# Layer norms and a projection in column tiles, the bf16 terms of the roots moved between partitions by small transfers

## The reference, cut to what matters

```
x += conv0(x)              # routed 1x1 conv, 3x3 depthwise, 1x1 conv (96 hidden channels)
x += conv1(x)
y  = layernorm(x);  x += attention(y)
y  = layernorm(x);  x += ffn0(y)         # 5/2-bit float operands
y  = layernorm(x);  x += fourier(y)      # 48 hidden; FFT over 3136 tokens, complex diagonal, ReLU, inverse, projection to 24
y  = layernorm(x);  x += ffn1(y)
layernorm(x) = (x - mean_c(x)) / sqrt(var_c(x) + 1e-5)      # over the 24 channels of a token
```

## Time and profile before

| | us |
|---|---|
| median of 3 runs | 2803.33 |
| lowest, highest run | 2799.18, 2808.28 |
| profiled execution, its time | 2798.5 |
| profiled execution, its span | 2796.5 |
| mean granted TensorE clock | 0.896 |

### The profile page before, as it was taken

The page is one execution under the profiler, slowest core; times in us unless marked ns, Lnnn a source line. Parts: engine busy times, 40 slices in busy tenths (PEclk is TensorE's granted clock), DMA queues, the critical chain, the costliest instruction groups (busy, mean ns, idle before and its releaser), DMA issues.

```text
span 2796.5 us, 46610 instructions
## 1 busy us (share of the span) xinstructions
PE 2463.6 (88%) x18624; PEld 1413.1 (51%) x18624; DVE 1950.9 (70%) x3622; ACT 1682.0 (60%) x2834; POOL 70.6 (3%) x123
## 2 busy tenths in 40 slices
PE   3867988999979998999989998999989998987776
PEld 1323433666436744664436644466436744673562
DVE  4765877785957887797866786876857888355243
ACT  2334445765667577765666567665667667657534
POOL 1000000000000000000000000000000000000000
PEclk9977989998989999999969998999979999787865
DMA  4001000100020001000010001000010000000000
GB/s 133 1 1 18 1 1 1 19 1 1 1 35 2 2 1 29 8 1 1 10 26 2 1 1 31 5 2 1 1 25 2 1 1 18 1 1 4 15 1 18
DMA packets 108582, 29.63 MB, mean 11 GB/s; under 512 B 104144, under 2 KB 104272, under 8 KB 107984
## 3 DMA queue, kind: packets, MB, share of 16 engines
q1 hardware_dynamic: 108368, 26.65, 4.7%
HBM read 17.00 MB, written 9.63 MB: 10 GB/s over the span
## 4 chain that ended last, share of the span: by engine, by line
PE 66%; DVE 15%; ACT 14%; issue 4%; SPq 1%; DMA 0%; ACTq 0%; DVEq 0%
PE P L664 12%; PE P L645 10%; PE P L709 7%; PE P L679 6%; PE P L857 4%; PE P L700 4%; DVE acc L1348 4%; PE P L898 4%; PE P L685 3%; PE P L870 3%; ACT H L1016 2%; PE P L882 2%; PE P L810 2%; DVE SQ L1483 1%; PE P L725 1%
## 5 line engine op out<-in xcount | busy, mean ns | idle before, releaser
L1348 DVE SCALAR_TENSOR_TENSOR acc<-H,Dm,acc 128x784 f32<-128x784 f32 x1024 | 991.6, 1026 | 119.9 <-ACT acc L1024 119.5
L645 PE MATMUL P<-T,Wk 96*128 96x448 f32 (+1 forms) x768 | 409.9, 618 | 68.5 <-ACT H L1016 46.5
L664 PE MATMUL P<-H,diag 64*64 64x392 f32 x4608 | 403.9, 500 | 1.5 <-ACT H L1016 0.8
L1016 ACT ACTIVATE H<-P,biasA 128x448 f32<-128x448 f32 (+1 forms) x384 | 238.6, 621 | 258.9 <-PE P L645 209.4
L664 PEld LDWEIGHTS P<-H,diag 64*64 64x64 f32 x4608 | 172.0, 135 | 214.8 <-issue 207.2
L709 PE MATMUL P<-T,pack_b 96*96 96x448 f32 x448 | 245.0, 638 | 34.1 <-DVE T L1444 19.0
L645 PEld LDWEIGHTS P<-T,Wk 96*128 96x128 f32 x768 | 132.5, 207 | 216.1 <-ACT H L1016 122.0
L679 PE MATMUL P<-acc,Wk 128*96 128x392 f32 x512 | 200.2, 538 | 14.6 <-ACT acc L1053 14.5
L1047 ACT ACTIVATE acc<-P,biasT 128x392 f32<-128x392 f32 x128 | 68.4, 584 | 204.1 <-PE P L664 204.0
L882 PE MATMUL P<-pack_b,arena 128*96 128x112 f32 x928 | 118.4, 280 | 30.7 <-DVE arena L1483 17.3
L679 PEld LDWEIGHTS P<-acc,Wk 128*96 128x96 f32 x512 | 87.3, 178 | 111.8 <-issue 111.2
(11 more groups left out here) (198 smaller groups left out, 4156.8 us busy)
## 6 DMA issues: line engine op xcount, KB each, us to landing
xin<-in_x SPq DMA_DIRECT2D x224, 42.0 KB, 2.2
out_y<-arena SPq DMA_DIRECT2D x8, 1176.0 KB, 5.7
pack_b<-in_pack_b SPq DMA_DIRECT2D x1, 3820.0 KB, 17.9
arena<-in_pack_s SPq DMA_DIRECT2D x1, 1780.0 KB, 9.0
pack_a<-in_pack_a SPq DMA_DIRECT2D x1, 1084.0 KB, 5.2
pack_i<-in_pack_i SPq DMA_DIRECT2D x1, 318.0 KB, 2.9
arena<-in_pack_k SPq DMA_DIRECT2D x1, 192.0 KB, 3.1
```

Source lines behind the costliest of these rows:

```text
L645: pe.matmul(conv_rows(slice(0, 128), H1B, m), Wk1[:, 128 * (u % NT):128 * (u % NT + 1)], image_rows(T[q % 3], a + r0, m), start=True, stop ...
L664: last = pe.matmul(conv_rows(slice(64 * h, 64 * (h + 1)), CVB + r, HH), diag[64 * r:64 * (r + 1), tap, :], H1[64 * r:64 * (r + 1), slot(s, ...
L1016: act.activation(H1[:, slot(s, j), o + r0:o + r0 + m, 1:1 + HW], conv_rows(slice(0, 128), H1B, m), ACT.Relu, bias=biasA[:, j, 1:2]).then_i ...
L1348: ins = ve.scalar_tensor_tensor(a, H1[:, slot(s, j), r:r + SR, c:c + HW], Dm[:, j, tap:tap + 1], a, ALU.mult, ALU.add)
```

## The change

- A variance chunk is four matmuls of 32 weight columns and 112 moving columns, into the four groups of 32 PSUM partitions. The variances of a norm stand as 128 x 112, and so do the root, the reciprocal and the three terms.
- The terms are no longer moved by VectorE. SyncE moves each of the three terms with four transfers (32 partitions x 112 bf16 values each) into `thirds`, 96 x 448: term k in partitions 32k to 32k+31. A chunk's spread is one bf16 matmul with 96 weight rows and 448 moving columns, and it waits for all twelve transfers.
- The projection of a frequency and image pair is two matmuls, of 64 and of 56 weight columns and 48 moving columns each, into PSUM partitions 0 to 63 and 64 to 119. A group holds 5 frequencies, so there are 6 groups for 8. `S2` and the constant `g` have 120 rows for 112.
- SyncE's program has the same three streams as the other engines and an order of its own in `TURNS`. The orders of all engines are written anew (TensorE's has 1508 turns for 1398, VectorE's 744 for 801, ScalarE's 1256 for 1211).
- GpSimd no longer clears four small buffers at the start. The pack with `selb` is smaller.

```
-LB = 14
-LN_N = TOK // LB
+LT = 4
+LN_N = CK // LT
+KR = 64 + HW
...
 TURNS = {
+    "sync": (
+        "d7 c11 m3 c3 m3 b3 c4 m2 c1 m1 c2 m3 b7 c4 m3 c3 b3 m3 b4 c4 m3 c3 b3 m3 b4 c4 m3 c3 b3 m3 b4 c4 m3 "
+        "c3 m3 b7 c3 m3 b3 m3 b4 m3 b3 m3 b8 "
+    ),
...
-        NX, NA, NW, NBI, NTR, NFO = 14, 12, 8, 8, 6, 7
+        NX, NA, NW, NBI, NTR, NFO = 14, 12, 6, 8, 6, 7
-            KG, KP = 4, 120
+            KG = 5
...
         @block.sync
+            def load(n):
+                if n >= XG:
+                    sp.wait_ge(in_tp.sem, n - XG + 1)
...
+            def conv_part(q):
+                for g in range(NCK):
+                    if q * NCK + g >= XG:
+                        yield
+                        load(q * NCK + g)
...
+            def shift_terms(q, norm, chain, before):
+                for k, made in enumerate((2, 4, 5)):
+                    yield
+                    sp.wait_ge(chain.sem, chain.at(q, before + made))
+                    for t in range(LT):
+                        sp.dma_start(norm.thirds[32 * k:32 * (k + 1), t, :],
+                                     norm.terms[k][32 * t:32 * (t + 1), :]).then_inc(norm.thirds_moved.sem, 16)
+            def middle(q):
+                yield from shift_terms(q, normM, chain_m, 0)
+                yield from shift_terms(q, normM, chain_m, 5 + 4)
+            def back(q):
+                yield from shift_terms(q, normB, chain_b, 0)
+                yield from shift_terms(q, normB, chain_b, 5 + NSG)
+                yield
+                sp.wait_ge(ot_ready.sem, ot_ready.at(q, NCK))
+                sp.dma_start(out_v[bass.ds(q * QI, QI), :, :].rearrange("b p f -> p b f"), xout).then_inc(out_stored.sem, 16)
...
                 def variance(c):
-                    for t in range(2):
-                        sq = LN_N * ((2 * c + t) % 4)
-                        last = pe.matmul(P[64 * t:64 * (t + 1), norm.var, 0:LN_N], par["selv"][0:R, o:o + 64],
+                    for t in range(LT):
+                        sq = CK * (c % 2) + LN_N * t
+                        last = pe.matmul(P[32 * t:32 * (t + 1), norm.var, 0:LN_N], par["selv"][0:R, o:o + 32],
                                          norm.SQ[:, sq:sq + LN_N], start=(c == 0), stop=(c == NCK - 1))
...
-                        pe.wait_ge(norm.rs_ready.sem, norm.rs_ready.at(q, i + 1))
+                        pe.wait_ge(norm.thirds_moved.sem, norm.thirds_moved.at(q, (i + 1) * 3 * LT * 16))
...
-                    for h in range(2):
-                        dst = P[0:R, norm.spread[c % NSP], LN_N * h:LN_N * (h + 1)]
-                        pe.matmul(dst, selb16[:, 2 * c + h, :], norm.rb2, start=True, stop=False)
-                        last = pe.matmul(dst, selb16[:, 2 * c + h, :], norm.rb3, start=False, stop=True)
-                    last.then_inc(norm.rs_psum.sem, 1)
+                    pe.matmul(P[0:R, norm.spread[c % NSP], 0:CK], selb16[0:96, c, :], norm.thirds[:, :, :].rearrange("p t n -> p (t n)"),
+                              start=True, stop=True).then_inc(norm.rs_psum.sem, 1)
...
-                            o = KP * (k % KG) + 2 * CH * j
-                            last = pe.matmul(P[0:2 * HW, B0 + g % BN, o:o + 4 * CH].rearrange("p (a n) -> p a n", a=2), UV[:, 2 * k + j, :],
-                                             twice, start=True, stop=True)
+                            o = R * (k % KG) + 2 * CH * j
+                            for p, a, n in ((0, 0, 64), (64, HW, HW)):
+                                last = pe.matmul(P[p:p + n, B0 + g % BN, o:o + 2 * CH], UV[:, 2 * k + j, a:a + n],
+                                                 par["fw2"][0:R, :], start=True, stop=True)
...
-                rest, third = norm.sdev, norm.rstd
-                link(ve.tensor_copy(norm.rb2, norm.rstd), q, half)
-                link(ve.tensor_tensor(rest, norm.rstd, norm.rb2, ALU.subtract), q, half)
-                link(ve.tensor_copy(norm.rmid, rest), q, half)
-                for h in range(2):
-                    ve.tensor_copy(norm.rb2[64 * h + 32:64 * h + 60, :], norm.rmid[64 * h:64 * h + 28, :])
-                link(ve.tensor_tensor(third, rest, norm.rmid, ALU.subtract), q, half)
-                ve.tensor_copy(norm.rb3[0:32, :], third[0:32, :])
-                ve.tensor_copy(norm.rb3[64:96, :], third[64:96, :]).then_inc(norm.rs_ready.sem, 1)
+                rest, (high, middle_, low) = norm.sdev, norm.terms
+                link(ve.tensor_copy(high, norm.rstd), q, half)
+                link(ve.tensor_tensor(rest, norm.rstd, high, ALU.subtract), q, half)
+                link(ve.tensor_copy(middle_, rest), q, half)
+                link(ve.tensor_tensor(low, rest, middle_, ALU.subtract), q, half)
```

More of the change, by code:

```diff
@@ L214, in __init__, with small @@
         self.n, self.D, self.SQ, self.cen, self.var, self.spread = n, D, SQ, cen, var, spread
+    def small(self, room, thirds):
+        self.sdev, self.rstd = room[:, 0:LN_N], room[:, LN_N:2 * LN_N]
+        terms = room[:, 2 * LN_N:2 * LN_N + 3 * LN_N // 2].bitcast(BF16)
+        self.terms = [terms[:, LN_N * k:LN_N * (k + 1)] for k in range(3)]
+        self.thirds = thirds
 class Ffn:
@@ L316, in build @@
         normM = Norm(n=0, D=Yf, SQ=z[0:R, 0:2 * CK], cen=(3,), var=4, spread=(3, 4))
[L317 to L320 removed]
+        normM.small(z[:, 2 * CK:], sb("thirdsm", [96, LT, LN_N], BF16))
         YT = z[0:BLK, 0:2 * BPG * (R + 1)].rearrange("p (b n) -> p b n", b=2 * BPG)
@@ L330, in build @@
         normB = Norm(n=2, D=Y, SQ=SQ[0:R, :], cen=(5, 6), var=7, spread=(5, 6, 7))
-        roots = sb("roots", [128, 2 * LN_N])
-        normB.sdev, normB.rstd = roots[:, 0:LN_N], roots[:, LN_N:]
-        normB.rmid = SQ[:, 0:LN_N // 2].bitcast(BF16)
-        normB.rb2, normB.rb3 = (sb(name, [128, LN_N], BF16)[:, :] for name in ("rb2b", "rb3b"))
+        roots = sb("roots", [128, CK])
+        normB.small(roots, sb("thirdsb", [96, LT, LN_N], BF16))
         T = Ts
@@ L426, in build @@
             norm.sd_ready = sig(f"deviation_ready_{half}", layers)
-            norm.rs_ready = sig(f"rstd_ready_{half}", layers)
+            norm.thirds_moved = sig(f"rstd_terms_moved_{half}", layers * 3 * LT * 16)
             norm.rs_psum = sig(f"rstd_in_psum_{half}", layers * NCK)
@@ L518, in _, with conv_end @@
         def _(sp):
-            def load(q, groups):
-                for g in groups:
-                    n = q * NCK + g
-                    if n >= XG:
-                        sp.wait_ge(in_tp.sem, n - XG + 1)
-                    o = BPG * (n % XG)
-                    for i in range(QI):
-                        src = x_v[q * QI + i, :, BPG * CH * g:BPG * CH * (g + 1)].rearrange("p (j c) -> p j c", c=CH)
-                        dma = sp.dma_start(xin[:, o:o + BPG, CH * i:CH * (i + 1)], src)
-                        dma.then_inc(xin_loaded[n % XG].sem, 16)
-            def store(q):
+            def load(n):
+                if n >= XG:
+                    sp.wait_ge(in_tp.sem, n - XG + 1)
+                o, g = BPG * (n % XG), n % NCK
+                for i in range(QI):
+                    src = x_v[n // NCK * QI + i, :, BPG * CH * g:BPG * CH * (g + 1)].rearrange("p (j c) -> p j c", c=CH)
+                    dma = sp.dma_start(xin[:, o:o + BPG, CH * i:CH * (i + 1)], src)
+                    dma.then_inc(xin_loaded[n % XG].sem, 16)
+            def conv_part(q):
[3 more added lines that the diff above has]
+                        load(q * NCK + g)
+            def conv_end(q):
+                yield
[12 more added lines that the diff above has]
+                yield from shift_terms(q, normB, chain_b, 5 + NSG)
+                yield
                 sp.wait_ge(ot_ready.sem, ot_ready.at(q, NCK))
@@ L536, in _ @@
                 sp.dma_start(pack_t[key], packs[key]).then_inc(par_loaded[key].sem, 16)
-            load(0, range(XG))
+            for n in range(XG):
+                load(n)
             for key in ("a", "s", "b"):
                 sp.dma_start(pack_t[key], packs[key]).then_inc(par_loaded[key].sem, 16)
-            for q in range(NQ):
-                load(q, range(XG, NCK))
-                if q + 1 < NQ:
-                    load(q + 1, range(XG))
-                if q >= 2:
-                    store(q - 2)
-            for q in range(max(NQ - 2, 0), NQ):
-                store(q)
+            for_quads("sync", conv_part, conv_end, middle, back)
             sp.wait_ge(out_stored.sem, 16 * (NQ + 1))
@@ L884, in fourier @@
                     last.then_inc(sp_psum.sem, 1)
-                twice = par["fw2"][0:R, :].unsqueeze(1).broadcast_to([R, 2, 2 * CH])
                 for g in range(NW):
@@ L911, in fourier @@
                         o = 2 * HW * (k % 4)
-                        last = pe.matmul(P[0:R, B0 + g % BN, o:o + 2 * HW], S2[:, k, :], par["g"][0:2 * HW, k, :],
+                        last = pe.matmul(P[0:R, B0 + g % BN, o:o + 2 * HW], S2[:, k, :], par["g"][0:KR, k, :],
```

(13 more changed lines are left out.)

30 lines of the change are left out of this document (13 added, 17 removed), and 213 rows, old and new, of the table TURNS.

## The result

The changed kernel takes 2868.84 us (median of 4 runs, 2865.96 to 2875.54) beside 2801.73 us for the kernel before on the same chip: a ratio of 1.0224, 95% interval 1.0191 to 1.0256. It is slower by 67 us by the medians and by 63 us by the ratio, where 2700 us were forecast. The profiled execution takes 2875.54 us, with a span of 2873.8.

The account below looks back on a forecast made before the run. TensorE was taken as nearly the bound (88% busy, 66% of the chain). Its matmuls -104, VectorE's norm work -14, late terms +14 us: -104 from 2798.5, forecast 2700 us, 8-in-10 range 2655 to 2780.

Parts of the forecast that it names:

- Rival (c): Terms come late and TensorE stands at each norm's first spread matmul: up to 157 us lost, 2842 us; chance 0.09.
- (d): With less to do, TensorE's mean granted clock falls by 0.02, costing 37 us: 2737 us; chance 0.10.
- the one on the root: Reciprocal to spread: VectorE's savings give 14 us; transfers add 3.6 us, bare in the last quad's four norms, 14 us lost.
- SyncE's queue: Input loads behind a norm's terms come at most some us late, covered by the ring of four chunks: no cost.
- The sum: TensorE's busy time falls by 54 (projection), 47 (spread) and 34 us (variances), 135 us together.
- The variances' term: Variance chunks as eight instructions, four at a time: 0.24 us for 0.38, saving 34 us at the mean clock.
- The projection's term: Projection as 1856 short matmuls at 30.0 ns, 56 us for 112.6: a saving of 54 us.
- L870's 30.0 ns: Time per instruction of an existing two-tile matmul (64 weight, 58 moving columns), taken as the new projection's price.
- Rival (a): Short matmuls are not cheap: projection at 63 ns an instruction, 32-column tiles only two at a time; 2771 us, chance 0.10.
- The 77%: Share of TensorE's 135 us saving that becomes time, midway between 66% of chain and 88% busy: 104 us.
- Rival (b): Co-bound: VectorE or ScalarE fill in, 0.4 of TensorE's 135 us is realised, 54 us: 2750 us; chance 0.16.
- the 15/70 of the step: VectorE's chain share over its busy share, turning 64 us less VectorE work in the norms into 14 us.

Follow-up runs that it names:

- experiment 1: Changed kernel with its new orders, the twelve transfers a norm replaced by twelve VectorE copies: 2733.67 us, ratio 0.9763.
- experiment 2: Kernel before with its own orders, plus the change's variances, spread and projection in tiles (groups of 4) and twelve VectorE copies: 2769.95 us, ratio 0.9890.
- experiment 3: Changed kernel with only the first term moved, by four transfers a norm, the second and third left out of the result: 2704.72 us, ratio 0.9659.
- experiment 7: Changed kernel with SyncE moving only the first term; VectorE copies the second and subtracts the third straight into place: 2732.98 us, ratio 0.9739.
- experiment 6: Changed kernel without transfers: VectorE copies the first two terms and subtracts the third straight into place: 2736.04 us, ratio 0.9753.

## Why the prediction was wrong

Rival (c) is what happened, with (d) on top. The step that failed is the one on the root: "TensorE has other streams' work in front of the wait as long as three quads are under way, and that hides it. It is bare where one quad's chain sets the end."

- **The cover.** The step took 4 of 32 norms as bare. In the trace TensorE waits in 31 of 32. Other streams' work does lie around, but TensorE executes its list strictly in order, and the list holds too little of it between the last variance and the first spread of a norm. The trace of the kernel before could have told this, norm by norm. There the spread starts 4.2 us after the reciprocal at the least, 5.3 us at the median, and later than 9.1 us in only 3 of the 32 norms. The step's own middle, 4.2 + 3.6 = 7.8 us, is later than 26 of them. Had each of these been held back to 7.8 us, that would be 65 us in all, and to 9.1 us 101 us (estimates, from the intervals in that trace), where the step took 14. The prediction never made this count, which is what decides (c).
- **The price.** The interval was to be 6.5 to 9.1 us, and 9.85 was measured. The step had 0.33 to 0.53 us an issue and eleven issues in a row. The rows of after have 7.47/12 = 0.62 us from one to the next. Landing was 1.7 us, near its bound of 1.8. So 5.65 us more in the last norm, where 3.6 was taken and 4.9 was the far end. Four norms of it are 23 us and would have been inside the range; 32 of them are 181 us. The waits for the terms grew by 127.9 us (19.0 to 146.9), so some 30% of it was covered.
- **SyncE's queue.** "An input load that stands behind a norm's terms comes at most some us late" looked at the wrong side. The terms stand behind the loads, and in the norm at 1221.51 the interval grew to 14.0 us by it. This is in five of the middle program's norms only, some 14 us beyond 9.9 us in all.
- **The clock.** (d) had a fall of 0.02, 37 us. The fall was 0.04, and the step in (d) named less work as the cause. With less work alone it fell by 0.015 (experiment 1). The other 0.025 came with the waits.
- **The matmuls.** The sum was right, two of its three prices were not. Experiment 1 shows them without the transfers' waits. Columns as above: its spread, its variances.

```profile
0.00:2880.00 2880.00, 81.01 (x224) 0.89 0.05 10
...
0.00:2880.00 2880.00, 92.88 (x1792) 36.42 (x1792) 0.89 0.05 10
```

  The spread saves 42.6 us (47 forecast), the variances 55.8 (34 forecast; the 47 of its bound was passed), the projection 37.9 (54 forecast). Together 136.3, where the sum had 135. That is luck: errors of 16 and 22 us cancelled. The variances' term was too small because it set 0.24 us against 0.38, although its own row gives 0.53 us for a chunk. The projection's term was too large because L870's 30.0 ns is a full-clock price: in the trace of before, all eight quads' L870 fell on the full clock. The rows of after have 30.9 ns in one stretch, but 56.4 ns in the other, and three of the eight quads' projections take 51 ns or more. In the last quad the projection took 14.4 us from start to end, not 7 to 10.
- **The Trainium skill's two rules on short matmuls.** At the full clock an instruction of the projection took 30.9 ns. By the Trainium skill's page "TensorEngine Tiling (Array Packing)", Instruction Overhead, it would be 25 ns (an estimate, its 60 cycles at 2.4 GHz). That is somewhat too low. By the Trainium skill's page "TensorE: Matmul & The Clock Gate" (on 56 ns and 53.3 ns) it would be 62 ns where the decoding isn't done in hardware. No quad's projection shows that: they take 30.9 to 57.3 ns, the highest at half the clock. Rival (a) is out.
- **The 77%.** Of experiment 1's 95.0 us less busy time, 70.1 us became span (74%), but only 95 of the 136 saved in the touched groups left TensorE at all. The rest went back into other matmuls, part of it by the lower clock, part perhaps only by how the records overlap. So the share that counts is 70/136, about a half, and it includes what the new orders gave. Under the old orders (experiment 2) it is 27/134, a fifth. Rival (b) with its 0.4 lay between.
- **VectorE.** Busy 1879.9 us, 1887 forecast: right. What it is worth stays open. The nearest pair is experiments 3 and 7, with the same four transfers and the same matmuls: 50 us less of VectorE's work and 28 us less time, more than the 15/70 of the step. Experiments 1 and 7 show nothing for 19 us less of it, with 8 us more of waiting.

With four transfers a norm, whose spread starts 4.79 us after the reciprocal, the kernel takes 2705 us, where 2700 were forecast. So the failed step is what kept the forecast from coming true, but that the rest comes so near is partly luck. The forecast took the new orders at nothing and the matmuls at 104 us. The runs show the orders worth 36 us with the copies, and the tiles and copies under the old orders worth 33 us of the median. No run has the new orders with the old tiles, so the two can't be told apart further.

Two things were not tried on the chip: one transfer for each term, and the twelve issues shared between two queues. The dose of 4, 8 and 12 suggests that either would pay; it isn't shown. Experiments 1, 6 and 7 do the whole computation and beat both kernels, by 2.4, 2.5 and 2.6% of the time before.

## What to carry to other kernels

When a step between two engines is handed to transfers, count the issues in the queue and multiply: twelve small ones in a row were 7.5 us, while twelve copies by an engine that had already made the data were 2.3 us. Before calling a longer latency hidden, list the interval from the producer's start to the waiting engine's first use for every occurrence in the trace before, and add up by how much the new latency exceeds each. A wait that recurs on the engine that bounds the kernel cost more here than its length: from 4 to 12 transfers 116 us of waiting and 170 us of span, as the clock fell with it.

## What the runs showed of the hardware that was not expected

- A transfer of 32 partitions x 224 bytes within the chip's memory lands 1.7 us after its issue (1.6 to 3.1 in the changed kernel) and holds SyncE's queue for about 0.6 us (median 590 ns, 507 at the least, 2002 at the most, in experiment 3). That is more than an output store's issue of 328 ns, although the store moves 1176 KB and the transfer 7 KB.
- A VectorE copy of 32 x 112 bf16 values to other partitions takes 181 ns, and twelve in a row 2.33 us.
- Four column tiles do run side by side. A chunk's variances in two tiles of 64 columns took 0.60 us at the full clock and 1.01 at half of it; the same sums in four tiles of 32 columns take 0.40 and 0.60 us (granted clock 1.00 and 0.50 in these stretches). Over the run that is 96.6 us for 148.7. First the kernel before, then the kernel after:

```profile
2744.45 1.01 PE L700 MATMUL P<-SQ,pack_b 96*64 96x224 f32 x4 [0.29 <-ACT SQ L1066]
...
1218.39 0.40 PE L725 MATMUL P<-mid,pack_b 96*32 96x112 f32 x8
...
2817.31 0.60 PE L725 MATMUL P<-SQ,pack_b 96*32 96x112 f32 x8 [0.70 <-ACT SQ L1088]
```

- The clock fell as TensorE's waiting grew: with the same instructions and orders its mean was 0.889 with 31 us of waits for the terms, 0.873 with 75 and 0.856 with 147.
